# Maxima step of one head, with parts of a sixth of a projection

## The reference, cut to what matters

```python
q = (query @ Wq + bq).reshape(b, l2, H, DH).transpose(0, 2, 1, 3)
k = (key @ Wk + bk).reshape(b, l1 + l2, H, DH).transpose(0, 2, 1, 3)
v = (value @ Wv + bv).reshape(b, l1 + l2, H, DH).transpose(0, 2, 1, 3)
score_prev = jnp.einsum('bhqd,bhkd->bhqk', q, k[:, :, :l1]) * SCALE
score_self = (q * k[:, :, l1:]).sum(-1, keepdims=True) * SCALE
score_prev = jnp.where(mask[:, None, None, :], score_prev, -jnp.inf)
weights = jax.nn.softmax(jnp.concatenate([score_prev, score_self], -1), axis=-1)
...
x = x + attn @ Wo + bo                       # L0
x = x + softmax((x + e) @ f.T) @ f           # L1
x = x + layernorm(x + relu(x @ W1 + b1) @ W2 + b2) * gamma + beta   # L2, adapter
x = x + (x @ A.T) @ B.T + lang               # L3, low rank
```

## Time and profile before

| | us |
|---|---|
| median of 3 runs | 1389.57 |
| lowest, highest | 1387.92, 1389.87 |
| profiled run, its own time | 1388.07 |
| its span, first to last instruction | 1386.2 |
| PE busy | 1304.2 (94%) |
| PE weight loads busy | 563.4 (41%) |
| DVE busy | 920.7 (66%) |
| ACT busy | 879.9 (63%) |
| POOL busy | 424.9 (31%) |

### The profile page before, as it was taken

How to read it: one execution, slowest core, us unless ns; L and a number is a source line. 1 busy time by engine, 2 the same in 40 slices (tenths; PEclk the granted TensorE clock), 3 DMA queues, 4 the chain that set the end, 5 groups by cost and what they waited for, 6 DMA issues and landing times.

```text
span 1386.2 us, 20006 instructions
## 1 busy us (share of the span) xinstructions
PE 1304.2 (94%) x7049; PEld 563.4 (41%) x7049; DVE 920.7 (66%) x1600; ACT 879.9 (63%) x1857; POOL 424.9 (31%) x372
## 2 busy tenths in 40 slices
PE   6889999999999999899998999989999999999995
PEld 3332463325533255333543236432463325533252
DVE  4686468864697556975478745896468854598544
ACT  3697447883388744886458853687447883388731
POOL 4431044410533106430165102641044410533114
PEclk9999999999999999999999999999999999999996
DMA  5303012030221202220021301213012130220100
GB/s 172 88 23 102 1 54 71 30 102 16 56 67 41 77 32 51 57 86 31 31 70 47 109 1 38 71 39 110 1 54 68 33 101 14 56 70 25 63 1 31
DMA packets 62161, 75.82 MB, mean 55 GB/s; under 512 B 14378, under 2 KB 35174, under 8 KB 62062
## 3 DMA queue, kind: packets, MB, share of 16 engines
q1 hardware_dynamic: 62000, 74.53, 18.8%
q10 hardware_dynamic: 62, 0.01, 0.0%
HBM read 40.81 MB, written 8.40 MB: 35 GB/s over the span
## 4 chain that ended last, share of the span: by engine, by line
PE 63%; ACT 19%; DVE 14%; issue 3%; POOL 1%; DMA 0%; ACTq 0%; POOLq 0%
PE bank L456 23%; PE banks L456 12%; ACT banks L744 9%; DVE nmx L1018 9%; ACT big L796 7%; PE bank L1362 6%; PE banks L1346 6%; PE bank L1199 6%; PE banks L1280 3%; PE bank L1309 2%; PE bank L1372 1%; PE bank L1314 1%; DVE prod L1008 1%; PE bank L1336 1%; DVE y L1064 1%
## 5 line engine op out<-in xcount | busy, mean ns | idle before, releaser
L744 ACT ACTIVATE banks<-banks,nmx 128x512 f32<-128x512 f32 x512 | 340.5, 671 | 55.6 <-DVE nmx L1018 53.2
L1018 DVE TENSOR_REDUCE nmx<-banks 128x1 f32<-128x512 f32 x512 | 325.9, 684 | 70.2 <-PE banks L1280 69.1
L796 ACT ACTIVATE big<-banks 128x1024 f32<-128x1024 f32 x256 | 247.3, 1022 | 43.6 <-PE banks L1346 42.5
L456 PE MATMUL bank<-fT,w_hi 128*128 128x512 f16 x768 | 246.9, 383 | 1.2 <-issue 1.1
L1280 PE MATMUL banks<-KQ 97*128 97x512 f16 x512 | 155.3, 385 | 38.6 <-ACT banks L744 36.5
L530 POOL TENSOR_TENSOR big<-x,b2r 128x512 f32<-128x512 f32 x32 | 40.6, 1269 | 412.2 <-DVE x L945 372.2
L1346 PE MATMUL banks<-KQ 98*128 98x512 f16 x512 | 141.0, 382 | 13.4 <-ACT big L796 8.4
L456 PE MATMUL bank<-fT,w_lo 128*128 128x512 f16 x384 | 147.3, 384 | 0.0
L491 POOL TENSOR_TENSOR half<-qk,ones 128x512 f16<-128x512 f32 x64 | 66.5, 1040 | 227.9 <-ACT qk L724 206.6
L1362 PE MATMUL bank<-big,V 128*32 128x512 f32 x1024 | 136.4, 605 | 0.0
L456 PEld LDWEIGHTS bank<-fT,w_hi 128*128 128x128 f16 x768 | 75.5, 98 | 93.3 <-issue 18.0
(11 more groups left out here) (149 smaller groups left out, 1968.2 us busy)
## 6 DMA issues: line engine op xcount, KB each, us to landing
KQ<-half SPq DMA_DIRECT2D x384, 64.0 KB, 2.0
tiles_in<-in_x_dram SPq DMA_DIRECT2D x32, 256.0 KB, 7.2
tiles_in<-in_fside_BxSxS_dram SPq DMA_DIRECT2D x32, 256.0 KB, 2.8
x<-in_x_dram SPq DMA_DIRECT2D x8, 1024.0 KB, 6.0
out_dram<-x SPq DMA_DIRECT2D x32, 256.0 KB, 2.0
w<-in_L_cond_W_dram SPq DMA_DIRECT2D x16, 256.0 KB, 4.6
b2r<-in_L_cond_b_dram SPq DMA_DIRECT2D x8, 256.0 KB, 4.4
gr<-in_L_cond_gamma_dram SPq DMA_DIRECT2D x8, 256.0 KB, 5.3
```

The costliest lines, as they stand in the source:

```text
L456: mm = eng.matmul(out_ap, pairs[n][0], pairs[n][1], start=(first and n == 0), stop=(last and n == len(pairs) - 1))
L744: ins = eng.activation(bank(step, i)[:, j % 2, :], bank(step, i)[:, j % 2, :], ACT.Exp, bias=nmx[:, t, h:h + 1], accum_out=esum[:, t, h:h ...
L796: eng.activation(big[:, n % 2, 2 * u:2 * u + 2, :], bank(step)[:, :, :], ACT.Exp).then_inc(read(step), 1)
L1018: eng.tensor_reduce(nmx[:, t, h:h + 1], bank(step, i)[:, j % 2, :], AX_X, ALU.max, negate=True).then_inc(max_done, 1)
```

## The change

A maxima step is now SMAX(g, u, v): one head, one bank of a pair. It has its own wait and increments on each engine. `free[k]` of a pair now counts heads; a head may be written when the head before the last in its pair has been read, which is the same bank one use ago (`wait_half_free`, count - 1). Only the first step on each pair in a batch waits for all earlier uses. `PARTS` becomes 6 (two matmuls a part), `OPEN` and `F16_AFTER` double, and an adapter step is placed behind every second slot. A stage so has 64 maxima steps.

```diff
--- before.py
+++ after.py
@@ -92,8 +92,8 @@
         return [("PART", n, step) for n in range(PARTS - 1)] + [step]
 
 
-    slots = [("IN", NT), ("IN", NT + 1), ("PART", 0, ("K", 0)), ("IN", NT + 2), ("PART", 1, ("K", 0)),
-             ("IN", NT + 3), ("K", 0)] + parts(("Q", 0)) + parts(("KS", 0))
+    slots = [("IN", NT), ("IN", NT + 1), *parts(("K", 0))[:2], ("IN", NT + 2), *parts(("K", 0))[2:4],
+             ("IN", NT + 3), *parts(("K", 0))[4:]] + parts(("Q", 0)) + parts(("KS", 0))
     for g in range(1, NG):
         slots += parts(("K", g)) + parts(("Q", g)) + parts(("KS", g))
     for kind in ("VS", "V"):
@@ -101,11 +101,11 @@
             slots += parts((kind, n))
 
     opens = [slots.index(("Q", g)) + OPEN[g] for g in range(NG)]
-    maxima = [("SMAX", g, u) for g in range(NG) for u in range(2 * NT)]
+    maxima = [("SMAX", g, u, v) for g in range(NG) for u in range(2 * NT) for v in range(2)]
     out, later = [], {}
     f16_at = slots.index(("KS", NG - 1)) + F16_AFTER
     for n in range(NT):
-        later[f16_at + 2 * n] = [("F16", n)]
+        later[f16_at + 4 * n] = [("F16", n)]
     rows = sums = False
     for i, step in enumerate(slots):
         out.append(step)
@@ -116,7 +116,7 @@
             out.append(("MROW",))
             rows = True
             late = i + PARTS
-        if adapters:
+        if adapters and i % 2 == 0:
             out += [a for a in (adapters.pop(0),) if a]
         if rows and not sums and i >= late and not adapters:
             out.append(("SROW",))
@@ -135,9 +135,9 @@
 
 
 
-OPEN = (16, 13, 13, 13)
-F16_AFTER = 6
-PARTS = 3
+OPEN = (32, 26, 26, 26)
+F16_AFTER = 12
+PARTS = 6
 WEIGHTS_AT = (("K", 0), ("Q", 1), ("K", 2))
 
 NORMS_AT = (5, 7, 8, 9)
@@ -173,7 +173,7 @@
             give(n % 2, step)
             n += 1
         elif step[0] == "SMAX":
-            give((4, 6)[m % 2], step)
+            give((4, 6)[m // 2 % 2], step)
             m += 1
         elif step[0] in ("MROW", "SROW"):
             give({"MROW": 4, "SROW": 6}[step[0]], step)
@@ -353,6 +353,11 @@
 
             k, c = place(step, b)
             eng.wait_ge(free[k], c)
+
+        def wait_half_free(eng, step, b):
+
+            k, c = place(step, b)
+            eng.wait_ge(free[k], c - 1)
 
         def wait_full(eng, step, b):
 
@@ -735,15 +740,12 @@
                         eng.activation(V[:, step[1], :], bank(step, i)[:, :], ACT.Copy, scale=1.0 / WS
                                        ).then_inc(read(step, i), 1)
                     elif kind == "SMAX":
-                        _, g, u = step
+                        _, g, u, v = step
                         t, q = divmod(u, 2)
-                        for j in (2 * q, 2 * q + 1):
-
-                            eng.wait_ge(max_done, b * MAXIMA + (g * 2 * NT + u) * 2 + j % 2 + 1)
-                            h = NG * j + g
-                            ins = eng.activation(bank(step, i)[:, j % 2, :], bank(step, i)[:, j % 2, :], ACT.Exp,
-                                                 bias=nmx[:, t, h:h + 1], accum_out=esum[:, t, h:h + 1])
-                        ins.then_inc(read(step, i), 1)
+                        h = NG * (2 * q + v) + g
+                        eng.wait_ge(max_done, b * MAXIMA + (g * 2 * NT + u) * 2 + v + 1)
+                        eng.activation(bank(step, i)[:, v, :], bank(step, i)[:, v, :], ACT.Exp, bias=nmx[:, t, h:h + 1],
+                                       accum_out=esum[:, t, h:h + 1]).then_inc(read(step, i), 1)
                     elif kind == "NEG":
 
                         wait_full(eng, ("SELF", NG - 1), b)
@@ -1009,14 +1011,12 @@
                                                  in1=qk32[:, g % 2, :], op0=ALU.add, op1=ALU.mult
                                                  ).then_inc(read(step, i), 1)
                     elif kind == "SMAX":
-                        _, g, u = step
+                        _, g, u, v = step
                         t, q = divmod(u, 2)
+                        h = NG * (2 * q + v) + g
                         wait_full(eng, step, b)
-
-                        for j in (2 * q, 2 * q + 1):
-                            h = NG * j + g
-                            eng.tensor_reduce(nmx[:, t, h:h + 1], bank(step, i)[:, j % 2, :], AX_X, ALU.max,
-                                              negate=True).then_inc(max_done, 1)
+                        eng.tensor_reduce(nmx[:, t, h:h + 1], bank(step, i)[:, v, :], AX_X, ALU.max, negate=True
+                                          ).then_inc(max_done, 1)
                     elif kind == "MROW":
 
 
@@ -1269,17 +1269,20 @@
                                             skip_group_check=True)
                         mm.then_inc(done(step, i), 1)
                     elif kind == "SMAX":
-                        _, g, u = step
+                        _, g, u, v = step
                         t, q = divmod(u, 2)
-                        if u == 0:
+                        j = 2 * q + v
+                        if u == v == 0:
                             eng.wait_ge(stacked[g], b * DMAS_PER_STACK + DMAS_PER_STACK)
                             if g == 0:
                                 eng.wait_ge(mask_in, b * 16 + 16)
-                        wait_free(eng, step, b)
-                        for j in (2 * q, 2 * q + 1):
-                            mm = eng.matmul(bank(step, i)[:, j % 2, :], KQ[0:SHIFT_ROW, j, g, 1, t * P:(t + 1) * P],
-                                            KQ[0:SHIFT_ROW, j, g, 0, :], start=True, stop=True)
-                        mm.then_inc(done(step, i), 1)
+                        if g == 0 and u < 2 and v == 0:
+                            wait_free(eng, step, b)
+                        else:
+
+                            wait_half_free(eng, step, b)
+                        eng.matmul(bank(step, i)[:, v, :], KQ[0:SHIFT_ROW, j, g, 1, t * P:(t + 1) * P],
+                                   KQ[0:SHIFT_ROW, j, g, 0, :], start=True, stop=True).then_inc(done(step, i), 1)
                     elif kind == "MROW":
 
                         eng.wait_ge(max_done, b * MAXIMA + MAXIMA)
@@ -1289,8 +1292,8 @@
                         mm.then_inc(done(step, i), 1)
                     elif kind == "SROW":
 
-                        wait_read(eng, ("SMAX", NG - 1, 2 * NT - 2), b)
-                        wait_read(eng, ("SMAX", NG - 1, 2 * NT - 1), b)
+                        wait_read(eng, ("SMAX", NG - 1, 2 * NT - 2, 1), b)
+                        wait_read(eng, ("SMAX", NG - 1, 2 * NT - 1, 1), b)
                         wait_free(eng, step, b)
                         for t in range(NT):
                             mm = eng.transpose(bank(step, i)[0:H, 0, t * P:(t + 1) * P], esum[:, t, :], ident[:, :])
```

## The result

The changed kernel takes 1379.89 us (median of 4 runs, 1377.38 to 1380.51) against 1388.74 us (1387.61 to 1389.87) for the kernel before beside it: 8.85 us or 0.64% faster, ratio 0.9936 [0.9923, 0.9948]. The forecast was 1383.1, a gain of 6.5. The profiled run is the lowest of the four (1377.38, span 1375.5); the spans of the other three are 1377.8 to 1378.6, so what the profile shows is the best case.

The account below looks back on a forecast made before the run. VectorE and ScalarE in turn were taken to bound the maxima stages. 4.2 us from seven middle batches plus 2.3 from the first made 6.5, off 1388.07: 1381.6, or 1383.1 as median; range 1370 to 1389.

Parts of the forecast that it names:

- Up to head 1.4: TensorE, middle batch, up to group 1, pair 4: no wait remains; the pair starts at 565.02 instead of 566.04.
- The copy of Q3: ScalarE, middle batch: it gets to Q3's copy at 564.8 against 565.73 before.
- GpSimd and the norm piece: Middle batch: three VectorE norm operations each end with a GpSimd operation, so the piece lasts 3.6 us instead of 2.17.
- the rival of the short stall: Norm piece starts before 566.65 and passes sooner: net 0.8 to 1.4 us more per batch, 1373 or 1377; chance 0.29.
- walk: Following one middle batch queue by queue from the first scores at 544.61: gain 0.6 us per middle batch, 4.2 in seven.
- the long stall: Likeliest case, chance 0.45: norm piece held through three GpSimd operations, head 1.5 0.35 us late; own range 1380 to 1386.
- To 1.5, 2.4 and the exponential there: Middle batch: head 1.5 reduced at 570.3, 2.4 at 582.75, its exponential starting at 583.47 instead of 583.74.
- The last heads: End of a middle batch's maxima stage: last head written at 599.95, 0.84 after 3.5's second-half exponential starts; before, 600.48.
- The new wait at the transposes: TensorE at the transposes of the maxima, since LORA3 moved behind them: a new wait of 0.5 us.
- Elsewhere at nothing: First norm piece group (GpSimd scaling some 1.5 us later, about 1.5 us of cover) and group 3's stacks: both at nothing.
- The first batch: ScalarE is the limit; refilling a bank at a time closes nine holes between exponentials, 2.3 us.
- Increments and waits at nothing: 256 more waits and increments on each of two engines cost nothing; the skill's 26.3 ns each would make 6.7 us.

Follow-up runs that it names:

- e1: Changed kernel with GpSimd's two additions of br issued earlier, at the squares, ahead of the split of Q3: 1369.15 us, ratio 0.9871.
- e12: Changed kernel with only the transposes of the maxima (MROW) one slot later: 1373.04 us, ratio 0.9894.
- e13: e9 with GpSimd's f16 split of the first input tile waiting until the second pair's first three norm operations are done: 1357.37 us, ratio 0.9775.
- e8: The changed kernel once more, word for word: 1379.86 us, ratio 0.9942 to the kernel before.
- e6: Kernel before with only GpSimd's two additions of br moved earlier, as in e1: 1386.75 us, ratio 0.9998.
- e7: e1 with the first head of each pair waiting until both heads of the pair's last use are read: 1375.41 us, ratio 0.9905.
- e9: e1 with MROW one slot later and VectorE's last-weight cast in two halves, behind KS2 and Q3 of the first batch: 1362.15 us, ratio 0.9812.
- e4: Kernel before with parts of a sixth and adapters in every second slot, but maxima steps still pairs of heads: 1386.50 us, ratio 0.9997.
- e2: Changed kernel with the first head of each pair waiting until both heads of its last use are read: 1392.08 us, ratio 1.0038.

## Why the prediction was right, and where it was not

The time was right within 3.2 us and the sign for the reason given. That the sum came so close is in part luck, as two misses stand against each other: the seven middle batches gave 2.9 and 2.4 us in the two profiles instead of 4.2, and the first batch more than the 2.3 forecast. Point by point, with times counted from the first score matmul of the stage (544.61 before, 536.05 after, so that forecast and run can be laid side by side):

1. *Up to head 1.4.* No wait remains near the old 0.92; the norm piece starts at 22.18, forecast 22.14. Right.
2. *The copy of Q3.* 20.22, forecast 20.19, before 21.12. Right.
3. *GpSimd and the norm piece.* Three operations of 1.16, 1.19 and 1.19 us, the last done at 25.79, forecast 25.79. Right, and by e1, e12 and e13 shown to be the cause of the wait behind it. The Trainium skill, "SBUF — State Buffer", section "Who interferes with whom", says that VectorE and GpSimd share a port pair as an exclusive lock, held by the one that issues first for its whole instruction. This case's trace agrees: held to the end of GpSimd's operation in the fourth batch of e12 (1.16 us), 0.16 us in the fifth, where GpSimd's operation is the longer one. The cost then hangs on a few nanoseconds between two starts (through at 15, held at 19 and more), and the rival of the short stall was a real one: e12 got it three times in seven, the profiles of the changed kernel in none of fourteen. The prediction decided between the two with a walk that it called no better than 0.15 us, so that the long stall came was right, but not something the walk could settle.
4. *To 1.5, 2.4 and the exponential there.* 25.70, 38.10 and 38.82 in the batches whose clock did not fall; forecast 25.69, 38.14 and 38.86. Right.
5. *The last heads.* Here the walk was 0.34 us short. The exponential of the second half of 3.5 starts at 54.26, forecast 54.5, but the last head is written at 55.68 instead of 55.34: heads are issued one slot apart, a score matmul and two of a projection, about 0.65 us, so the last one is not written as soon as its bank is free. The new wait at the transposes is 0.50 as forecast, and the attention stage starts at 63.76, forecast 63.49, before 64.09. In the stage the gain is 0.33 instead of 0.6.
6. *Elsewhere at nothing.* In the opening a wait of 0.34 us ahead of a projection matmul (at 523.27 before) is gone, which the sum did not have. These two misses work against each other: 0.74 per batch without a fall of the clock, forecast 0.6.
7. *The clock.* Not in the prediction. It forecast that TensorE's wait would grow from 1.81 to 2.4 us, and charged the wait alone. Behind it the granted clock fell to the 1.2 GHz level in four and in five of seven batches, which brings the mean from 0.74 down to 0.41 (profiled run) and 0.35 (e8): 2.9 and 2.4 us in the middle batches instead of 4.2.
8. *The first batch.* The holes between exponentials are gone. Behind the opening wait and at an equal clock the batch gained 2.8 us (e6 against e8), forecast 2.3; by e7 against e1 1.3 of it are the half counts, to which the prediction gave all, and the rest is the order. On top come 0.7 us of the opening wait and what the clock gives back behind it, and the landing of the cast moves the whole by 2.4 from one profile to the next. The prediction counted the opening wait (3.4) among the waits and then gave it no further thought; by e9 it was worth 3.3 us for a move of two instructions.
9. *Increments and waits at nothing.* The Trainium skill, "TensorE: Matmul & The Clock Gate", section "The cost: per-tile semaphore tail", gives for packed tiles the figure that the prediction cited, 26.3 ns for each increment. The full matmuls of this trace show nothing of that size: in batches whose clock stayed full a score matmul, each with an increment, is followed by a projection matmul after 215 to 227 ns, and one projection matmul by the next after 215 to 226. The walk without a term for them is also met within 0.04 us at 2.4, but TensorE waits on the way, which could hide them. No run isolates them.
10. *What the change is worth.* The prediction had 0.6 per batch as the difference of a gain of 1.0 and a loss of 1.4. The runs say it more plainly: with the loss taken out (e1), the change gives 2.0 us per batch, 18 in all; 0.56 of the 2.0 are the half counts (e7), the rest the finer order.

The half counts alone were never run on the order of before, so how much they would give there is open. It also stays open why the clock fell behind some waits of 2.42 us and not behind others; the three kinds of period (no fall, a small loss, a large one) came back in the same turn in both profiles of after, so it does not look like chance, but no run tests what decides it.

## What to carry to other kernels

When a reordering puts a GpSimd operation beside small VectorE operations on SBUF, price them at the GpSimd operation's length, and look for the wait or the earlier step that keeps them apart; here that was worth more than the change itself (10.7 us in e1 and 4.8 in e13, against 8.85). Finer parts alone brought nothing (e4); steps of one head did, once the stall was out, and counts as fine as the steps added 0.56 us per batch to them (e7, e1). Read the opening of the first batch by itself, and compare it in several runs before a difference there is given to a change.

## What the runs showed of the hardware

- In the maxima stages TensorE's granted clock fell to the 1.2 GHz level behind some waits of 2.4 to 2.5 us (4 of 7 in the profiled run of the change, 5 of 7 in e8, 2 of 4 in e12, and 7 of 7 in e2, where one of 0.6 stood before it) and behind all those of 2.3 to 3.4 in the openings of the first batch, and never behind waits of 1.81 us or less. Batches with a fall were 0.07 to 0.86 us longer than those without.
- Two maxima from PSUM took 1.28 us beside GpSimd and no less without it; operations of 2 columns on SBUF took 0.16 alone and up to 1.19 beside it. Two casts of 1024 columns took 1.22 each alone (e9) and 3.20 to 4.14 together beside GpSimd's splits (e6, e1). It goes the other way too: where the cast had started 0.06 us ahead, GpSimd's first half of a split took 2.07 instead of 1.04 (e6).
- In e12 VectorE's operation started 15 ns behind GpSimd's in three batches and took 0.16 us, and 19 to 21 ns behind it in four and took 1.16.
